# Value columns laid group last, four apart, in a windowed-attention and FFN kernel

## The chip, the cores and the metric

The kernel runs on one core of one Trainium2 chip. The metric is the device time of one launch in microseconds (us), the median of several executions. The engines of the core are TensorE (PE, with its weight loads shown apart as PEld), VectorE (DVE), ScalarE (ACT), GpSimd (POOL) and SyncE (SP), which here does nothing but issue DMAs; ACT issues some too. 16 DMA engines move the data of both queues.

## What is computed

`x` is (4, 2048, 256) in fp32, 8192 tokens in all. One transformer layer is applied:

```python
x = x + attn(layernorm(x), Wq, Wk, Wv, Wo)   # 16 heads of 16, token i sees tokens i-63 .. i
x = x + ffn(layernorm(x), W1, b1, W2, b2)    # ternary W1 (1024x256) and W2 (256x1024), relu
# attn: q, k, v = x @ W.T; softmax(q k / 4 + bias) v; then @ Wo.T
```

## The kernel before

Precision comes from splitting: a value is held as a high and a low f16 part, and products are summed over the parts. That holds for the projections, for the values (`vd[..., v, ...]`, v = 0 high, 1 low) and for the softmax weights (`th`, `tl`).

The tokens go in 16 chunks of 512. Each chunk takes 16 slots (`for n in SLOTS`), and every engine's program is written out slot by slot with the tables `A_T`, `A_Q`, `Q_DMA`, `V_DMA` and so on. Stage A (`a_t`, `a_qk`, `a_v`) of a chunk runs in the slots before its attention, attention takes one slot per unit of 4 query blocks of 4 heads (`scores(n)`, `exps`, `turn`, `low`), and stage C (`wo`, `c_t`, `c_f`, `c_y`: output projection and FFN) follows after it. PE thus mixes, in every slot, scores of this chunk with stage C of the last and stage A of the next.

The 16 heads are four groups g of four heads h, head 4g + h, each of 16 columns d. Attention of a group, `values(gg)`, multiplies with block-diagonal stationary operands: `vb[b]` has, on partitions 32h to 32h+31, the values of head h for 32 tokens in the columns of h, and zeros elsewhere, so that one 128x128 f16 load serves the four heads of group g with both parts. It is 36 matmuls (32 in a batch's first chunk), th and tl in turn, each of 96 columns save four of 64 and four of 32, and each with its own weight load.

The way of the values: PE writes a chunk's V in two banks (line 1042), ACT and DVE copy high and low parts to `vd` (lines 559 and 786; a row of `vd` is a token), and then SP spreads them to `vb` by `place_v` (line 304): 16 DMAs of 32 KB written per chunk, for m in 0..3 and h in 0..3. SP's queue is in order. Its DMAs per chunk in that order are

- 16 of `place_v` (V), from slot 17 counted from the chunk before; the first waits until DVE has written the low parts of V;
- 8 of `place_q` for t = 1 (line 284), slot 20, and 2 of `place_k` for t = 1 (line 263), slot 22, called k1 below: the keys of groups 2 and 3, which `scores` of group 2 need at slot 8 of the chunk. The matmul that waits there is the first of that slot, the mask of line 967 (line 963 in a batch's first chunk);
- 12 of `place_q` and 4 of `place_k` for t = 0, for the chunk that follows (lines 284, 266, 268).

ACT's queue issues meanwhile the spreading of the softmax denominators (`parked`, `rwide`, lines 464 and 470), the loads of `x` for the sixth chunk ahead (line 478, 512 KB, until x has been read) and the stores (line 475).

The rows of Wv are transposed on PE in the set-up, and `weights` on ACT and DVE copies them to `wT["v"]` (lines 495 and 679).

Of the kernel before, what the change touches and what calls it, by code (L numbers as in the profile page):

```python
# [14 lines left out]
WS = 256.0  # L15
# [107 lines left out]
def build(nc, x_d, wq_d, wk_d, wv_d, wo_d, w1_d, b1_d, w2_d, b2_d, identf_d, maskf_d, smask_d, kmask_d, out_d):  # L123
    f32, f16, b16 = mybir.dt.float32, mybir.dt.float16, mybir.dt.bfloat16
    ALU, ACT, AX = mybir.AluOpType, mybir.ActivationFunctionType, mybir.AxisListType
# [4 lines left out]
    with ExitStack() as ctx:  # L130
        def sb(name, shape, dt):
            return ctx.enter_context(nc.sbuf_tensor(name, shape, dt))
# [10 lines left out]
        wT = {n: [sb(f"w{n}{p}", [128, 2, 256], f16) for p in "hl"] for n in "qkvo"}  # L143
# [28 lines left out]
        qm = sb("qm", [128, 2, 16 * 128], f16)  # L172
        ks = [sb(f"k{g}", [128, 1 + g // 2, 64 + CH], f16) for g in range(4)]
        kw = [sb(f"kw{g}", [128, 16, 96], f16) for g in range(2)]
        vd = sb("vd", [128, 4, 4, 2, 4, 16], f16)
        vb = [sb(f"vb{i}", [128, 4, 4, 4, 2, 4, 16], f16) for i in range(3)]
        pr = [sb(f"p{i}", [128, 384], f32) for i in range(NP)]
        pt = [sb(f"pt{i}", [128, 384], f32) for i in range(3)]
        negm = [sb(f"negm{i}", [128, 4], f32) for i in range(4)]
# [17 lines left out]
        banks = [ctx.enter_context(nc.psum_tensor(f"ps{i}", [128, 512], f32)) for i in range(8)]  # L197
# [24 lines left out]
        s_ex, s_ahi, s_chi = sem("s_ex"), sem("s_ahi"), sem("s_chi")  # L222
# [17 lines left out]
        def a_bank(c, w):  # L240
            return banks[TURN["A", c, w - 8 * c][0]]
# [51 lines left out]
        @block.sync  # L293
        def _(e):
            def place_v(c, m):
                b = c % 3
                e.wait_ge(s_alo, 8 * c + 6)
                e.wait_ge(s_zv, min(c, 2) + 1)
                if c >= 3:
                    e.wait_ge(s_pv, 4 * (c - 1))  # L300
                for h in range(4):
                    src = vd[32 * m:32 * m + 32, :, :, :, h, :].rearrange("p t g v d -> p (t g v) d")
                    dst = vb[b][32 * h:32 * h + 32, m, :, :, :, h, :].rearrange("p t g v d -> p (t g v) d")
                    e.dma_start(dst, src).then_inc(d_v[b], 16)  # L304

            e.dma_start(xs[0][:, 0:2, :], x_t[0][:, 0:2, :]).then_inc(d_x[0], 16)
            e.dma_start(identf[:, :], identf_d).then_inc(d_id, 16)
            e.dma_start(kmask, kmask_d).then_inc(d_km, 16)
            e.dma_start(smask, smask_d).then_inc(d_s, 16)
            for t in range(2):  # L310
                e.dma_start(nat["q"][:, t, :], wq_d[128 * t:128 * t + 128].rearrange("(g r) d -> r g d", g=2)
                            ).then_inc(d_w["q"], 16)
            for n, d in (("k", wk_d), ("v", wv_d)):
                e.dma_start(nat[n], d.rearrange("(t p) d -> p t d", p=128)).then_inc(d_w[n], 16)
            e.dma_start(pr[1][:, :], maskf_d).then_inc(d_m, 16)
            e.wait_ge(s_bz, 1)
            for r in (0, 32):
                e.dma_start(bt[0][r:r + 1, :], b1_d.rearrange("(a n) -> a n", a=1)).then_inc(d_b, 16)
                e.dma_start(bt[1][r:r + 1, :], b2_d.rearrange("(a n) -> a n", a=1)).then_inc(d_b, 16)
            e.dma_start(n1, w1_d.rearrange("(t p) d -> p t d", p=128)).then_inc(d_w["1"], 16)  # L320
            e.dma_start(n2, w2_d.rearrange("(t p) f -> p t f", p=128)).then_inc(d_w["2"], 16)
            for n in SLOTS:
                for t in range(2):
                    c = spread(n, Q_DMA[t], A_Q[t] + 2)
                    if c is not None:
                        place_q(e, c, t, ((0, 1, 2, 3), (0, 1, 2, 3), (0, 1, 2, 3) if c or t else (2, 3)))
                    c = spread(n, K_DMA[t], A_K[t] + 2)
                    if c is not None:
                        place_k(e, c, t, (0, 1) if c or t else (1,))
                c = spread(n, V_DMA, 17)  # L330
                if c is not None:
                    for m in range(4):
                        place_v(c, m)
# [125 lines left out]
        def _(e):  # L459
# [31 lines left out]
            def weights(ws):  # L491
                for w in ws:
                    n, t = "qkvo"[w // 2], w % 2
                    e.wait_ge(s_wp, w + 1)
                    e.activation(wT[n][0][:, t, :], banks[4 + w % 4][:, 0:256], ACT.Copy,
                                 scale=WS * (0.25 if n == "q" else 1.0)).then_inc(s_whi, 1)

            def magnitudes(j):
# [55 lines left out]
            def a_v(c, u):  # L554
                w = 8 * c + 4 + u
                e.wait_ge(s_a, w + 1)
                if c >= 1:
                    e.wait_ge(d_v[(c - 1) % 3], 256 * ((c - 1) // 3 + 1))
                e.activation(vd[:, 2 * u:2 * u + 2, :, 0].rearrange("p t g h d -> p (t g) (h d)"),
                             a_bank(c, w)[:, :].rearrange("p (a b) -> p a b", b=64), ACT.Copy, scale=1 / WS).then_inc(s_ahi, 1)  # L560

            def o_copy(gg):
                e.wait_ge(s_pv, gg + 1)
# [12 lines left out]
            for n in SLOTS:  # L576
# [24 lines left out]
                c = stage_c(n, X_DMA)  # L601
# [3 lines left out]
                for u in range(2):  # L605
                    c = stage_c(n, OUT_DMA[u])
# [11 lines left out]
                for h in range(2):  # L618
                    c = stage_c(n, C_T[h] + 1)
                    if c is not None:  # L620
                        c_t(c, h)
                    for f in range(4):
                        c = stage_c(n, C_F[h] + f + 1)
                        if c is not None:
                            c_f(c, h, f)
                for t in range(2):
                    c = stage_a(n, A_T[t] + 1)
                    if c is not None:
                        a_t(c, t)
                    c = stage_a(n, A_Q[t] + 1)  # L630
                    if c is not None:
                        a_q(c, t)
                    c = stage_a(n, A_K[t] + 1)
                    if c is not None:
                        a_k(c, t)
                    c = v_at(n - 1, t)
# [4 lines left out]
                for u in range(2):  # L641
                    c = norm_at(n, A_NORM[u], N_NORM[u])
# [6 lines left out]
        def _(e):  # L649
# [24 lines left out]
            def weights(ws):  # L674
                for w in ws:
                    n, t, bank = "qkvo"[w // 2], w % 2, banks[4 + w % 4]
                    hi, lo, src = wT[n][0][:, t, :], wT[n][1][:, t, :], bank[:, 0:256]
                    e.wait_ge(s_whi, w + 1)
                    e.scalar_tensor_tensor(out=lo, in0=src, scalar=WS * (0.25 if n == "q" else 1.0), in1=hi,
                                           op0=ALU.mult, op1=ALU.subtract).then_inc(s_wlo, 1)  # L680
# [100 lines left out]

            def a_v(c, u):
                w = 8 * c + 4 + u
                hi, lo = (vd[:, 2 * u:2 * u + 2, :, v].rearrange("p t g h d -> p (t g) (h d)") for v in range(2))
                e.wait_ge(s_ahi, w + 1)
                e.scalar_tensor_tensor(out=lo, in0=a_bank(c, w)[:, :].rearrange("p (a b) -> p a b", b=64),
                                       scalar=1 / WS, in1=hi, op0=ALU.mult, op1=ALU.subtract).then_inc(s_alo, 1)

            def o_add(gg):
# [40 lines left out]
            for n in SLOTS:  # L830
# [27 lines left out]
                for u in range(2):  # L858
                    c = stage_c(n, C_WO[u] + 1)
                    if c is not None:  # L860
                        residual(c, u, f"wo{u}")
                    c = stage_c(n, C_T[u] + 1)
                    if c is not None:
                        c_t(c, u)
                    for f in range(4):
                        c = stage_c(n, C_F[u] + f + 1)
                        if c is not None:
                            c_f(c, u, f)
                    c = stage_c(n, C_Y[u] + 2)
                    if c is not None:  # L870
                        residual(c, u, f"y{u}")
                for t in range(2):
                    c = stage_a(n, A_T[t] + 1)
                    if c is not None:
                        a_t(c, t)
                    c = stage_a(n, A_Q[t] + 1)
                    if c is not None:
                        a_q(c, t)
                    c = stage_a(n, A_K[t] + 1)
                    if c is not None:  # L880
                        a_k(c, t)
                    c = v_at(n - 1, t)
# [4 lines left out]
                for u in range(2):  # L887
                    c = norm_at(n, A_STATS[u], N_STATS[u])
# [4 lines left out]
                    c = stage_c(n, C_STATS[u])  # L893
# [4 lines left out]
        def _(e):  # L898
# [80 lines left out]
            def values(gg):  # L979
                c, g = gg // 4, gg % 4  # L980
                e.wait_ge(s_lo, 4 * gg + 4)
                e.wait_ge(d_v[c % 3], 256 * (c // 3 + 1))
                if gg >= 1:
                    e.wait_ge(s_osum, gg)
                else:
                    e.wait_ge(s_alo, 6)
                k0 = 0 if c % PER_BATCH == 0 else -2
                for k in range(k0, 16):
                    i0, i1 = max(k, 0), min(k + 3, 16)
                    off, num = 64 * i0 + 32 * k + 64, i1 - i0  # L990
                    lhs = vb[(c if k >= 0 else c - 1) % 3][:, k % 4, k % 16 // 4, g].rearrange("p v h d -> p (v h d)")
                    for tt in (th, tl):
                        rhs = tt[gg % 2][:, off:off + 64 * num].rearrange("p (a b) -> p a b", b=64)[:, :, 0:32]
                        ins = e.matmul(pvbank[:, 32 * i0:32 * i1], lhs, rhs, start=(k == k0 and tt is th),  # L994
                                       stop=(k == 15), skip_group_check=True)
                ins.then_inc(s_pv, 1)
# [111 lines left out]
            for n in SLOTS:  # L1108
# [19 lines left out]
                for h in range(2):  # L1128
                    c = stage_c(n, C_WO[h])
                    if c is not None:  # L1130
                        wo(c, h)
                    c = stage_c(n, C_T[h])
                    if c is not None:
                        c_t(c, h)
                    for f in range(4):
                        c = stage_c(n, C_F[h] + f)
                        if c is not None:
                            c_f(c, h, f)
                    for t in range(2):
                        c = stage_c(n, C_Y[h] + t)  # L1140
                        if c is not None:
                            c_y(c, h, t)
                for t in range(2):
                    c = stage_a(n, A_T[t])
                    if c is not None:
                        a_t(c, t)
                    c = stage_a(n, A_Q[t])
# [49 lines left out]
```

## Time and profile before

| | |
|---|---|
| Median of 3 runs | 757.39 us (755.42 to 757.71) |
| The profiled execution | 753.48 us, its span 751.7 us |
| Mean granted TensorE clock | 0.955 of full speed |
| PE busy | 669.8 us (89%) |
| DVE, ACT, POOL busy | 609.6, 569.0, 556.7 us (81, 76, 74%) |
| DMA packets | 511041, of them 479684 under 512 bytes |

A busy share is a mean over stages. A matmul's own time in the trace is its way through the array (some 200 ns for 96 columns); what a matmul costs in a stream is the distance from one start to the next. A DMA-issuing instruction has a duration on its queue as well: the time until the queue takes up the next.

### The profile page before, as it was taken

To read this page: it belongs to the slowest core of one execution; us is meant where nothing else is said; L and a number is where in the kernel's file an instruction comes from. 1 tells how busy PE (TensorE), PEld (TensorE's weight loads), DVE (VectorE), ACT (ScalarE), POOL (GpSimd) and SP (SyncE) were. 2 spreads that over 40 slices of the span, in tenths; PEclk is the share of its full clock that TensorE was granted. 3 is DMA by queue.
4 is the path that set the end of the run, shared out by engine and by line. 5 is a ranking of instruction groups with operands and counts; after the bars stand their busy time and mean duration, and the time that the engine had idled before them with its cause. 6 is when DMAs were issued, how large, how long until landed. Compare 5 with 4: busy or idle time off the path is not lost.

```text
span 751.7 us, 23901 instructions
## 1 busy us (share of the span) xinstructions
PE 669.8 (89%) x8048; PEld 569.0 (76%) x8048; DVE 609.6 (81%) x1391; ACT 569.0 (76%) x2489; POOL 556.7 (74%) x823
## 2 busy tenths in 40 slices
PE   7588798998979899898989989898997999897888
PEld 5456687887868687786868878686886878786776
DVE  5679798896969889598978969798896989797844
ACT  5768797896878789597868959787785989877722
POOL 7367898795868779487877958687695888788741
PEclk9769899999999999899999999999999999999999
DMA  8766666576655757656575775557476465665110
GB/s 270 106 84 95 112 80 96 86 95 123 72 94 77 122 90 92 122 66 103 77 120 88 92 124 72 93 78 122 85 90 116 56 103 82 91 90 89 34 43 29
DMA packets 511041, 70.59 MB, mean 94 GB/s; under 512 B 479684, under 2 KB 502470, under 8 KB 510920
## 3 DMA queue, kind: packets, MB, share of 16 engines
q1 hardware_dynamic: 478456, 42.43, 45.2%
q10 hardware_dynamic: 32464, 26.63, 13.7%
q8 instruction: 65, 1.06, 0.6%
q14 instruction: 56, 0.46, 0.2%
HBM read 20.25 MB, written 9.44 MB: 39 GB/s over the span
## 4 chain that ended last, share of the span: by engine, by line
PE 53%; SPq 18%; DVE 9%; DMA 8%; POOL 5%; issue 5%; ACT 2%; ACTq 0%; POOLq 0%; DVEq 0%
PE ps L1095 12%; PE ps L994 9%; SPq L304 9%; SPq L284 9%; PE ps L974 7%; DMA k<-kst 7%; PE ps L1083 6%; PE ps L1056 5%; PE ps L1031 4%; PE ps L1042 4%; DVE negm L718 2%; POOL tl L419 2%; PE ps L967 2%; PE ps L1068 1%; POOL osum L391 1%
## 5 line engine op out<-in xcount | busy, mean ns | idle before, releaser
L520 ACT ACTIVATE p<-ps,negm 128x96 f32<-128x96 f32 x1024 | 335.6, 355 | 18.6 <-DVE negm L718 18.6
L419 POOL TENSOR_TENSOR tl<-pt,th 128x384 f16<-128x384 f32 x256 | 234.1, 914 | 20.7
L520 ACT ACTIVATION_READ_ACCUMULATOR p<-ps,negm 128x1 f32 x1024 | 227.1, 222 | 0.0
L718 DVE TENSOR_REDUCE negm<-ps 128x4 f32<-128x384 f32 x256 | 138.6, 542 | 95.4 <-PE ps L974 91.5
L417 POOL CAST th<-pt 128x384 f16<-128x384 f32 x256 | 129.1, 504 | 86.0 <-DVE pt L735 83.3
L735 DVE STREAM_TRANSPOSE pt<-p 128x384 f32<-128x384 f32 x256 | 143.3, 560 | 2.4 <-ACT p L520 2.2
L974 PE MATMUL ps<-k,qbd 128*128 128x96 f16 x1536 | 127.5, 210 | 0.0
L974 PEld LDWEIGHTS ps<-k,qbd 128*128 128x128 f16 x1536 | 107.7, 100 | 11.4 <-issue 0.4
L994 PE MATMUL ps<-th,vb 128*128 128x96 f16 (+1 forms) x1120 | 109.5, 213 | 1.9 <-issue 1.9
L994 PE MATMUL ps<-tl,vb 128*128 128x96 f16 (+1 forms) x1120 | 108.8, 213 | 0.0
L994 PEld LDWEIGHTS ps<-th,vb 128*128 128x128 f16 x1120 | 102.5, 105 | 2.2 <-issue 2.0
L994 PEld LDWEIGHTS ps<-tl,vb 128*128 128x128 f16 x1120 | 101.6, 105 | 0.0
L1083 PE MATMUL ps<-xTCh,w1T 128*128 128x256 f16 x512 | 97.6, 272 | 0.8 <-ACT xTCh L568 0.8
L564 ACT ACTIVATE ohalf<-ps 64x512 f32<-64x512 f32 x64 | 37.9, 592 | 72.1 <-PE ps L994 71.5
L573 ACT ACTIVATE hTh<-ps 128x512 f16<-128x512 f32 x128 | 78.7, 615 | 16.5 <-PE ps L1083 16.0
L827 DVE SCALAR_TENSOR_TENSOR hTl<-ps,hTh 128x512 f16<-128x512 f32 x128 | 86.8, 679 | 3.0 <-ACT hTh L573 3.0
L1083 PE MATMUL ps<-xTCl,w1T 128*128 128x256 f16 x256 | 69.8, 272 | 1.3 <-DVE xTCl L820 1.2
L967 PE MATMUL ps<-maskf,identb 128*128 128x256 bf16 x120 | 33.0, 275 | 42.0 <-DMA k<-kst 40.1
L1083 PE MATMUL ps<-xTCl,w1L 128*128 128x256 f16 x256 | 69.8, 273 | 0.0
L1095 PE MATMUL ps<-w2T,hTl 128*128 128x256 f16 x512 | 66.5, 273 | 0.2 <-DVE hTl L827 0.2
L1095 PE MATMUL ps<-w2T,hTh 128*128 128x256 f16 x512 | 66.5, 273 | 0.0
L974 PE MATMUL ps<-kw,qm 128*128 128x96 f16 x512 | 61.3, 211 | 0.0
(141 smaller groups left out, 1439.5 us busy)
## 6 DMA issues: line engine op xcount, KB each, us to landing
k<-kst SPq DMA_DIRECT2D x32, 288.0 KB, 3.7
vb<-vd SPq DMA_DIRECT2D x256, 32.0 KB, 2.9
rwide<-parked ACTq DMA_DIRECT2D x32, 256.0 KB
out<-x ACTq DMA_DIRECT2D x32, 256.0 KB, 2.9
qbd<-qs SPq DMA_DIRECT2D x254, 32.0 KB, 2.5
x<-in_L_attn_hidden ACTq DMA_DIRECT2D x15, 512.0 KB, 5.3
kw<-kst SPq DMA_DIRECT2D x31, 192.0 KB, 4.6
k<-kst SPq DMA_DIRECT2D x31, 144.0 KB, 4.2
```

The costliest lines, as they stand in the source:

```text
L284: e.dma_start(bass.AP(tensor=to[:, :, :].tensor, offset=(32 * h + v) * 4096 + 32 * h, ap=[[2 * 4096, 16], [128, 32], [1, 32]]), qst[t][32 ...
L417: e.tensor_copy(th[g % 2][:, o], pt[n % 3][:, :]).then_inc(s_hp, 1)
L419: e.tensor_tensor(tl[g % 2][:, o], pt[n % 3][:, :], th[g % 2][:, o], ALU.subtract).then_inc(s_lo, 1)
L520: ins = e.activation(p[:, 96 * u:96 * u + 96], bank[:, 96 * u:96 * u + 96], ACT.Exp, bias=m[:, u:u + 1], accum_out=r[:, u:u + 1])
L573: e.activation(hT[0][:, 2 * f:2 * f + 2, :].rearrange("p a b -> p (a b)"), c_bank(c, f"f{h}{f}")[:, :], ACT.Relu).then_inc(s_chi, 1)
L718: e.tensor_reduce(negm[n % 4][:, :], sbank[n % 3][:, 0:384].rearrange("p (a b) -> p a b", b=96), AX.X, ALU.max, negate=True).then_inc(s_mx, 1)
L735: e.transpose(pt[n % 3][:, :], pr[n % NP][:, :]).then_inc(s_tr, 1)
L827: e.scalar_tensor_tensor(out=lo, in0=c_bank(c, f"f{h}{f}")[:, :], scalar=0.0, in1=hi, op0=ALU.max, op1=ALU.subtract).then_inc(s_cdv, 1)
L974: ins = e.matmul(bank[:, 96 * u:96 * u + 96], to[:, g % 2, 128 * blk:128 * blk + 128], keys, start=(g < 2 and not first and m == 0 and u = ...
L994: ins = e.matmul(pvbank[:, 32 * i0:32 * i1], lhs, rhs, start=(k == k0 and tt is th), stop=(k == 15), skip_group_check=True)
L1083: ins = e.matmul(bank[:, o], w, xTC[xp][:, k, :], start=(xp + k == 0), stop=(xp + k == 2))
L1095: ins = e.matmul(bank[:, o], hT[hp][:, f, t * 128:(t + 1) * 128], w2T[:, f, :], start=False, stop=(f == 7 and hp == 1))
```

## The change

In `vd` and `vb` the group g becomes the last dimension, behind the head's columns d; high and low part, head and column stand ahead of it. A row of `vd` is then, for each token tile t and part v, 256 elements in the order (h, d, g), where it was (g, h, d) with the parts between. For a head h, all four groups and 16 columns of a part lie side by side: 64 elements, 128 bytes. Before they were runs of one group, 16 elements, 32 bytes. `place_v` names the same elements, in 8 runs of 128 bytes for each of 32 partitions instead of 32 runs of 32 bytes.

So that stage A writes V in that order at once, the columns of `wT["v"]` are put into the order (h, d, g) in the set-up, with writes four elements apart; the copies of V from PSUM to `vd` then have rows of 256 on both sides. The stationary operand of `values` is now read from `vb` with elements four apart (8 bytes) instead of side by side. The instructions of each engine, their order and their waits stay as they were.

```diff
-        vd = sb("vd", [128, 4, 4, 2, 4, 16], f16)
-        vb = [sb(f"vb{i}", [128, 4, 4, 4, 2, 4, 16], f16) for i in range(3)]
+        vd = sb("vd", [128, 4, 2, 4, 16, 4], f16)
+        vb = [sb(f"vb{i}", [128, 4, 4, 2, 4, 16, 4], f16) for i in range(3)]
...
-                    src = vd[32 * m:32 * m + 32, :, :, :, h, :].rearrange("p t g v d -> p (t g v) d")
-                    dst = vb[b][32 * h:32 * h + 32, m, :, :, :, h, :].rearrange("p t g v d -> p (t g v) d")
+                    src = vd[32 * m:32 * m + 32, :, :, h].rearrange("p t v d g -> p (t v) (d g)")
+                    dst = vb[b][32 * h:32 * h + 32, m, :, :, h].rearrange("p t v d g -> p (t v) (d g)")
...
-                    e.activation(wT[n][0][:, t, :], banks[4 + w % 4][:, 0:256], ACT.Copy,
+                    hi, src = wT[n][0][:, t, :], banks[4 + w % 4][:, 0:256]
+                    if n == "v":
+                        hi, src = hi.rearrange("p (a g) -> p g a", g=4), src.rearrange("p (g a) -> p g a", g=4)
+                    e.activation(hi, src, ACT.Copy,
...
-                e.activation(vd[:, 2 * u:2 * u + 2, :, 0].rearrange("p t g h d -> p (t g) (h d)"),
-                             a_bank(c, w)[:, :].rearrange("p (a b) -> p a b", b=64), ACT.Copy, scale=1 / WS).then_inc(s_ahi, 1)
+                e.activation(vd[:, 2 * u:2 * u + 2, 0].rearrange("p t h d g -> p t (h d g)"),
+                             a_bank(c, w)[:, :].rearrange("p (a b) -> p a b", b=256), ACT.Copy, scale=1 / WS).then_inc(s_ahi, 1)
...
-                hi, lo = (vd[:, 2 * u:2 * u + 2, :, v].rearrange("p t g h d -> p (t g) (h d)") for v in range(2))
+                hi, lo = (vd[:, 2 * u:2 * u + 2, v].rearrange("p t h d g -> p t (h d g)") for v in range(2))
...
-                    lhs = vb[(c if k >= 0 else c - 1) % 3][:, k % 4, k % 16 // 4, g].rearrange("p v h d -> p (v h d)")
+                    lhs = vb[(c if k >= 0 else c - 1) % 3][:, k % 4, k % 16 // 4, :, :, :, g].rearrange("p v h d -> p (v h d)")
```

DVE's part of the set-up and of `a_v` changes in the same way as ACT's.

## Rows read from the trace of the kernel before

**Rows 1.** The page: the span, and busy time, share and instructions of each engine

```profile
span 751.7 us, 23901 instructions
...
PE 669.8 (89%) x8048; PEld 569.0 (76%) x8048; DVE 609.6 (81%) x1391; ACT 569.0 (76%) x2489; POOL 556.7 (74%) x823
```

**Rows 2.** The waits of PE: us in total, times, the longest

```profile
PE ps L967 <- DMA k<-kst: 40.1, 12, 4.8
PE ps L963 <- DMA k<-kst: 12.2, 3, 4.6
```

**Rows 3.** Windows from one V burst to the next: length, busy by engine, clock, DMA share, GB/s

```profile
103.69:146.66 42.97, 40.27 (x501) 34.71 (x500) 36.62 (x85) 34.36 (x155) 34.27 (x51) 0.96 0.59 85
...
235.23:277.39 42.16, 38.59 (x494) 33.28 (x492) 36.65 (x85) 34.53 (x156) 33.61 (x51) 1.00 0.67 99
...
542.41:587.65 45.24, 40.61 (x496) 35.01 (x495) 36.79 (x85) 34.79 (x156) 33.63 (x51) 0.96 0.62 93
587.65:627.75 40.10, 38.60 (x494) 33.26 (x492) 36.00 (x83) 34.52 (x156) 33.64 (x51) 1.00 0.62 92
```

**Rows 4.** The timeline of SP's queue, chunks 8 and 13: start, us, DMAs issued

```profile
365.66 13.89 SPq L304 DMA_DIRECT2D vb<-vd  x16
379.65 8.06 SPq L284 DMA_DIRECT2D qbd<-qs  x8
387.83 1.47 SPq L263 DMA_DIRECT2D k<-kst  x2
...
587.65 14.00 SPq L304 DMA_DIRECT2D vb<-vd  x16
601.75 5.35 SPq L284 DMA_DIRECT2D qbd<-qs  x8
```

**Rows 5.** The chain that ended last, from 380 to 396 us: start, us, what

```profile
387.83 3.54 DMA k<-kst
...
391.50 0.32 PE ps L963
...
392.44 2.40 PE ps L994 x32
```

**Rows 6.** Lines 304, 284 and 263 by source line: ns of one issue, min/median/max

```profile
L304 SPq DMA_DIRECT2D vb<-vd x256: 585/668/3903, 34.3 to 679.6; - x128
...
L284 SPq DMA_DIRECT2D qbd<-qs x254: 585/630/3417, 17.4 to 687.0; - x127
...
L263 SPq DMA_DIRECT2D k<-kst x32: 567/584/611, 32.9 to 688.3; - x32
```

**Rows 7.** The page, DMA queues: packets, MB, share of 16 engines' span

```profile
q1 hardware_dynamic: 478456, 42.43, 45.2%
```

**Rows 8.** SP's queue (q1) in 370 to 374, 383.4 to 387.2 and 389.2 to 391.4 us

```profile
q1 hardware_dynamic: 4490, 0.14, 50.9%
...
q1 hardware_dynamic: 2838, 0.18, 47.3%
...
q1 hardware_dynamic: 261, 0.48, 94.0%
```

**Rows 9.** The timeline of ACT's queue in chunk 8

```profile
376.92 0.37 ACTq L478 DMA_DIRECT2D x<-in_L_attn_hidden  x1
```

**Rows 10.** The timeline of PE in one group of `values`: start, us, matmul

```profile
359.99 0.18 PE L994 MATMUL ps<-th,vb 128*128 128x32 f16 x1
360.02 0.18 PE L994 MATMUL ps<-tl,vb 128*128 128x32 f16 x1
...
360.27 0.21 PE L994 MATMUL ps<-th,vb 128*128 128x96 f16 x1
360.31 0.21 PE L994 MATMUL ps<-tl,vb 128*128 128x96 f16 x1
```

**Rows 11.** The chain from 330 to 400 us: a whole group of `values` at full clock

```profile
369.54 1.40 PE ps L994 x36
```

**Rows 12.** Groups of weight loads, shapes apart: busy us, mean ns of one, idle before

```profile
L994 PEld LDWEIGHTS ps<-th,vb 128*128 128x128 f16 x1120 | 102.5, 105 | 2.2 <-issue 2.0 <-POOL tl L419 0.2
...
L1020 PEld LDWEIGHTS ps<-identf,xnA 128*128 128x128 f32 x128 | 15.4, 147 | 0.7 <-DVE wvl L679 0.6
```

More of the change, by code:

```diff
@@ L677, in weights @@
                     hi, lo, src = wT[n][0][:, t, :], wT[n][1][:, t, :], bank[:, 0:256]
+                    if n == "v":
+                        hi, lo = (z.rearrange("p (a g) -> p g a", g=4) for z in (hi, lo))
+                        src = src.rearrange("p (g a) -> p g a", g=4)
                     e.wait_ge(s_whi, w + 1)
@@ L783, in a_v @@
                 w = 8 * c + 4 + u
-                hi, lo = (vd[:, 2 * u:2 * u + 2, :, v].rearrange("p t g h d -> p (t g) (h d)") for v in range(2))
+                hi, lo = (vd[:, 2 * u:2 * u + 2, v].rearrange("p t h d g -> p t (h d g)") for v in range(2))
                 e.wait_ge(s_ahi, w + 1)
-                e.scalar_tensor_tensor(out=lo, in0=a_bank(c, w)[:, :].rearrange("p (a b) -> p a b", b=64),
+                e.scalar_tensor_tensor(out=lo, in0=a_bank(c, w)[:, :].rearrange("p (a b) -> p a b", b=256),
                                        scalar=1 / WS, in1=hi, op0=ALU.mult, op1=ALU.subtract).then_inc(s_alo, 1)
```

## The prediction

> **What bounds the kernel now.** I read the page's first part, then PE's waits, then windows cut at the start of each V burst, then SP's queue, then the chain through one wait.
>
> PE is the busiest engine, 669.8 of 751.7 us, and DVE follows with 609.6 [rows 1]. Of the 82 us in which PE is idle, one cause holds 52.3: 40.1 us in 12 waits and 12.2 in 3 at the mask matmul of group 2, released by the DMA of k1 [rows 2]. That is one wait in nearly every chunk, 3.5 us on the mean, 4.8 at most. The windows show that PE loses nothing else of size. A full chunk costs PE 38.6 us of busy time where the granted clock was 1.00 [rows 3], and one whose clock fell costs about 40.5, since the clock drops to 0.5, the lower of its two levels, right behind a wait: the 32 matmuls of `values` after the one at 391.50 took 2.40 us [rows 5], where a whole group of 36 takes 1.40 [rows 11]. Over the 11 windows from 103.69 to 587.65 PE is busy for 442.2 us (40.2 each, first and last in [rows 3]), and 11 times 38.6 is 424.6: the low clock costs 17.6 us beside the waits.
>
> Why k1 is late shows in SP's queue. In chunk 8 the V burst starts at 365.66 (V's low parts have just been written), 16 V and 8 q issues take until 387.71, k1 is issued behind them at 387.83 [rows 4], lands 3.54 us later, and PE goes on at 391.50 [rows 5]. PE had been ready at 387.78, by its idle time of 3.72. So from the burst's start to k1 in place it is 25.7 us, and PE's own work fills 22.1. The wait is what the queue takes beyond that.
>
> **What the change does to SP's queue.** A V DMA had 32 partitions with 32 runs each, 1024 packets; now it has 256, and they hold four times the bytes. Over 256 DMAs 262144 of the queue's 478456 packets [rows 7] become 65536. Two things follow.
>
> *The issue itself.* Undisturbed issues take 668 ns for V (1024 runs), 630 for q (512 runs of 64 bytes) and 584 for k (128 long runs) [rows 6]. With 256 runs I put V at 600, by those three. Sixteen of them save 16 x 0.068 = 1.1 us a chunk.
>
> *The stalls.* Undisturbed, 16 V and 8 q issues with gaps of 40 ns would take 16 x 0.71 + 8 x 0.67 = 16.7 us. They take 22.0 in chunk 8, and 19.4 in chunk 13, behind which no x is loaded [rows 4]. So 2.7 to 5.3 us a chunk are single issues that stick, up to 3.9 us [rows 6]. In chunk 8 one falls together with the 512 KB of x issued at 376.92 on the other queue [rows 9]. How much of that lies on V's packets? From 370 to 374 us nearly all packets are V's: 4 us x 16 engines x 0.509 / 4490 = 7.3 ns for 32 bytes. In the q stretch it is 3.8 x 16 x 0.473 / 2838 = 10.1 ns, mostly for 64 bytes, and in the k1 stretch 2.2 x 16 x 0.94 / 261 = 127 ns for about 1800 bytes [rows 8]. The price is largely by the packet. 128 bytes should cost about 12 ns, an estimate between the second and third. One V DMA then holds each DMA engine for 16 x 12 = 0.2 us instead of 64 x 7.3 = 0.47, of 0.71 us from issue to issue. Behind a load of x the queue would be caught up sooner, but the load's own time stays. The bounds are no relief (0) and all of it (5.3). I take half, 2.6, since both V's backlog and x's transfer hold the queue and no row parts them.
>
> Together k1 lands 3.7 us earlier in a chunk (bounds 1.1 and 6.4). The waits of 52.3 us, each shortened by 3.7, leave about 4 us on the longest ones: a gain of 48. With no wait of size the clock has no reason to drop; of the 17.6 us I count 15. Before 103.69 and behind 587.65 I count no clock.
>
> *What is late next.* DVE is busy for 36.7 us of a chunk and PE will need 38.6 [rows 3]. That is little room, and DVE feeds the exponentials that free PE's score banks. That a chunk of 40.10 us ran with no other wait of size on PE [rows 3] shows that the others keep up to there; for the last 1.5 us no row does. I take off 0.4 us a chunk, 6 in all. Sum: 48 + 15 - 6 = 57.
>
> **What it does to the weight loads.** 2240 loads of `vb` now read elements 8 bytes apart. Today such a load costs nothing: in a group, 32-column matmuls start about 27 ns apart and 96-column ones 42 ns [rows 10], so a load takes at most some 27 ns and hides behind its neighbour. The 36 make 1.40 us [rows 11]. No row shows a strided load. A gain is excluded, since matmuls of 96 columns are already paced by their columns. If it takes up to 40 ns, only the eight narrow ones of a group grow, 8 x 13 ns x 64 groups = 7 us at most. The upper bounds: the only slower kind of load in the trace is that of f32, 147 ns in length against 105 [rows 12]. If a load's pace grew by those 42 ns, to 69, a group would take 36 x 0.069 = 2.5 us, or 70 us over 64 groups. If loads did not overlap at all, 36 x 0.105 = 3.8 us, it would be 153 us. I take zero: the room from 27 to 42 ns covers a read that is half again as slow, and the f32 load moves twice the bytes, which this does not.
>
> The trace is silent on strides, so the Trainium skill is weighed here. "SBUF — State Buffer" (Door 1, the note on cachelines) says that accesses within one 16-byte line run at full rate as long as two or more fall on a line; four f16 apart are exactly two. "TensorE: Matmul & The Clock Gate" (Weight-path perf modes) says that the fast load works packed or strided, but also that it reads 32 bits at a time instead of one element. If the second half of that ruled, a load would double to an estimated 54 ns, and a group would take 1.94 us: 35 us over all groups, and about 735 as the time. That stands as a rival below; no run here has shown it yet.
>
> **The rest.** The copies to `vd` have as many elements as before, with longer rows; the set-up's four strided copies happen once. The clearing of `vb` is the same size. I count nothing for them; the copies run under PE's work, and 0.1 us more in each would delay each V burst by as much.
>
> **The sum.** 753.5 (the profiled execution's own time) - 57 = 696.5. That execution was 3.9 us under the median of the runs, so the forecast is 757.4 - 57 = 700.
>
> **The rivals.**
> - *The stalls stay* (the queue sticks on the other queue's transfers alone). Then k1 gains 1.1 us a chunk: 16.5 us of waits and a few of clock, 738. For it: the longest issues coincide with x. Against: the price by the packet. "DMA: Bandwidth & Descriptors" (Why small descriptors are slow) of the Trainium skill speaks for it, and further: between SBUF and SBUF small descriptors cost nothing extra, so nothing but bytes would count, and the time would stay near 757. The rows disagree, with 4.4 bytes a ns at 32 bytes, 6.3 at 64 and 14 at 1800. Chance 0.12, with 0.03 of it for no change at all.
> - *Loads a little over the pace*, 45 to 60 ns a load. At 54 the group takes 1.94 us, plus 35 us against a gain of now 57 to 60: about 733. PE's own work between V burst and k1 grows too, so that waits vanish more surely. Chance 0.12.
> - *The weight loads become the bound*: over 62 ns a load (57 us over 64 groups are 0.89 us each, 2.29 / 36 = 64 ns) the kernel is slower than before. At 69 ns it is 757 + 70 - 63 = 764, at 105 ns 757 + 153 - 66 = 844. Middle 790. For it: the reads are no longer side by side, and every one of the 2240 is hit. Against: the room from 27 to 42 ns, and that bytes read are the same. Chance 0.14.
> - *DVE or ACT takes PE's place* at the higher rate: chunks stay at 40.1 as in window 587.65, instead of 38.6 plus 0.7. Then 13 chunks gain about 1 us less each: 713. It is in the likeliest case's range.
>
> **How the numbers follow.** Forecast case 0.62, its own range 686 to 718 (from all waits and 17.6 us of clock gone, 757 - 70 = 687, to chunks of 40.1 or a load at 40 ns). The range for 8 in 10 reaches to the stalls staying, 742, and takes in the loads a little over the pace; below it starts at 684. What is left out is the bound by weight loads and some of the edges. A difference of 0.3% (2.3 us) is about what a measurement of this kernel can tell from no change. Faster by more than that: 0.62 + 0.09 + 0.12 = 0.83. Within it: 0.03. Slower: 0.14.
>
> **What will show it.** SP's timeline: V issues with a median near 600 ns, and 16 V plus 8 q in 18 to 19 us. Packets of its queue near 282000. PE's waits for k1 under 10 us in total, the granted clock near 1.00 from 100 us on, chunk windows near 39.3 us. A group of `values` still at 1.40 us, with 27 ns between the narrow starts. The prediction falls if that group is over 1.5 us, or if the V and q issues still take 21 us.

## The result, and the profile after

The changed kernel takes 693.31 us (median of 4 runs, 691.04 to 696.39), the kernel before 756.4 us in the runs beside it. The ratio is 0.9175, with a 95% interval of 0.9127 to 0.9223. The forecast was 700. The profiled execution of the changed kernel took 696.39 us, with a span of 694.6. Some executions of the kernel before are slower than the rest; the ratios leave them out, so a ratio can say a little less than the medians beside it.

The page of the changed kernel, its span and busy times (against [rows 1]), and the packets of SP's queue (against [rows 7]):

```profile
span 694.6 us, 23901 instructions
...
PE 653.9 (94%) x8048; PEld 557.4 (80%) x8048; DVE 611.0 (88%) x1391; ACT 567.7 (82%) x2489; POOL 556.4 (80%) x823
...
q1 hardware_dynamic: 281848, 42.43, 38.7%
...
k<-kst SPq DMA_DIRECT2D x32, 288.0 KB, 4.0
```

The span fell by 57.1 us. PE's busy time fell by 15.9 of them and its idle time, span less busy, from 81.9 to 40.7. Packets fell by 196608, as counted. The last row is k1's time from issue to landing, 4.0 us where the page of before has 3.7: k1 did not land sooner after its issue, it was issued sooner.

PE's waits in the changed kernel (against [rows 2]):

```profile
PE ps L973 <- DMA k<-kst: 4.5, 5, 2.8
PE ps L969 <- DMA qbd<-qs: 4.3, 1, 4.3
PE ps L973 <- ACT p L523: 3.5, 4, 1.2
...
PE ps L1062 <- POOL oTl L399: 3.0, 2, 1.7
PE ps L1000 <- DVE osum L800: 1.6, 1, 1.6
...
PE ps L969 <- DMA k<-kst: 1.0, 1, 1.0
```

Of 52.3 us for k1, 5.5 are left. The other rows are small, 1 to 3.5 us each for ACT, POOL and DVE, and most of them stood in the kernel before at 1 to 3 us.

Windows from V burst to V burst (against [rows 3]; length, busy by engine, clock, DMA share, GB/s):

```profile
102.74:141.84 39.10, 38.90 (x502) 33.68 (x501) 36.66 (x85) 34.53 (x156) 34.54 (x52) 1.00 0.53 94
...
337.71:377.79 40.08, 39.12 (x496) 33.66 (x495) 36.83 (x85) 34.72 (x156) 33.61 (x51) 1.00 0.55 105
377.79:416.55 38.76, 38.70 (x494) 33.38 (x493) 36.47 (x85) 34.45 (x156) 33.65 (x51) 1.00 0.58 108
...
534.26:573.62 39.36, 38.70 (x494) 33.39 (x493) 36.02 (x83) 34.47 (x156) 33.55 (x51) 1.00 0.51 93
```

Full chunks take 38.8 to 40.1 us where all but one of [rows 3] took 42 to 46, at the full granted clock, and PE is busy for nearly all of it. PE is now the bound in the plain sense.

The timeline of SP's queue in chunks 8 and 13, counted from 0 as in [rows 4]:

```profile
337.71 11.66 SPq L304 DMA_DIRECT2D vb<-vd  x16
349.47 7.11 SPq L284 DMA_DIRECT2D qbd<-qs  x8
356.70 1.48 SPq L263 DMA_DIRECT2D k<-kst  x2
...
534.26 11.95 SPq L304 DMA_DIRECT2D vb<-vd  x16
546.30 6.22 SPq L284 DMA_DIRECT2D qbd<-qs  x8
```

The issue of V's DMAs by source line, ns min/median/max (against [rows 6]):

```profile
L304 SPq DMA_DIRECT2D vb<-vd x256: 585/611/1993, 35.7 to 623.4; - x128
```

From the burst's start to the end of q it is 18.9 us in chunk 8, where it was 22.0, and 18.3 in chunk 13, where it was 19.4. Chunk 8 is the slowest of the changed kernel. Over the ten chunks in which ACT's queue loads x during that stretch (3 to 12) the mean is 18.2 us where it was 22.1; over the full ones without such a load (2, 13, 14 and 15) it is 18.0 where it was 19.3. So the load of x hardly shows any more. The longest V issue is 1993 ns, where it was 3903.

The timeline of PE in one group of `values`, at its start and its end (against [rows 10]):

```profile
302.44 0.18 PE L1000 MATMUL ps<-th,vb 128*128 128x32 f16 x1
302.46 0.18 PE L1000 MATMUL ps<-tl,vb 128*128 128x32 f16 x1
...
303.82 0.19 PE L1000 MATMUL ps<-th,vb 128*128 128x32 f16 x1
303.86 0.18 PE L1000 MATMUL ps<-tl,vb 128*128 128x32 f16 x1
```

The chain that ended last, through a whole group of the changed kernel (against [rows 11]):

```profile
302.60 1.44 PE ps L1000 x36
```

The narrow matmuls (32 and 64 columns) start about 32 ns apart over the four pairs (27 before), the wide ones 42 as before, and the group takes 1.44 us instead of 1.40.

### The profile page after: what moved, and what is told of

Same layout as the page of the kernel before. It is cut to its first block, busy times and chain, and to the rows that moved or that the text cites. A ratio compares the mean times of both kernels' runs of the same rounds, so it can differ in the third digit from the quotient of the medians.

```text
span 694.6 us, 23901 instructions
## 1 busy us (share of the span) xinstructions
PE 653.9 (94%) x8048; PEld 557.4 (80%) x8048; DVE 611.0 (88%) x1391; ACT 567.7 (82%) x2489; POOL 556.4 (80%) x823
## 3 DMA queue, kind: packets, MB, share of 16 engines
q1 hardware_dynamic: 281848, 42.43, 38.7%
## 4 chain that ended last, share of the span: by engine, by line
PE 69%; SPq 7%; POOL 6%; DVE 6%; DMA 5%; ACT 4%; issue 3%; ACTq 0%; POOLq 0%; DVEq 0%
PE ps L1101 14%; PE ps L1089 11%; PE ps L1000 10%; PE ps L980 9%; PE ps L1037 8%; PE ps L1062 6%; PE ps L1048 4%; SPq L284 4%; DMA k<-kst 3%; SPq L304 3%; POOL tl L419 2%; PE ps L973 2%; PE ps L1074 2%; ACT p L523 2%; PE ps L1026 2%
## 5 line engine op out<-in xcount | busy, mean ns | idle before, releaser
L419 POOL TENSOR_TENSOR tl<-pt,th 128x384 f16<-128x384 f32 x256 | 234.4, 916 | 20.7
L980 PE MATMUL ps<-k,qbd 128*128 128x96 f16 x1536 | 125.6, 207 | 0.0
L980 PEld LDWEIGHTS ps<-k,qbd 128*128 128x128 f16 x1536 | 106.1, 99 | 11.1 <-issue 0.3
L1000 PE MATMUL ps<-th,vb 128*128 128x96 f16 (+1 forms) x1120 | 100.5, 205 | 2.2 <-DVE osum L800 1.6
L1000 PE MATMUL ps<-tl,vb 128*128 128x96 f16 (+1 forms) x1120 | 100.5, 205 | 0.0
L1000 PEld LDWEIGHTS ps<-th,vb 128*128 128x128 f16 x1120 | 96.4, 115 | 2.8 <-issue 1.7
L1000 PEld LDWEIGHTS ps<-tl,vb 128*128 128x128 f16 x1120 | 95.8, 115 | 0.0
L391 POOL TENSOR_TENSOR osum<-osum,rwide 128x512 f32<-128x512 f32 x32 | 40.6, 1268 | 22.1 <-DVE osum L800 21.4
```

Source lines behind the costliest of these rows:

```text
L419: e.tensor_tensor(tl[g % 2][:, o], pt[n % 3][:, :], th[g % 2][:, o], ALU.subtract).then_inc(s_lo, 1)
L980: ins = e.matmul(bank[:, 96 * u:96 * u + 96], to[:, g % 2, 128 * blk:128 * blk + 128], keys, start=(g < 2 and not first and m == 0 and u = ...
```

## The experiments

In four of them (quarter, half, step1 and step8) and in smallx part of the computation is left out or replaced, as their expectations say.

**quarter**: the packets of the changed kernel without its layout, and a quarter of its bytes.

```diff
 # the kernel before
-src = vd[32 * m:32 * m + 32, :, :, :, h, :]
-dst = vb[b][32 * h:32 * h + 32, m, :, :, :, h, :]
+src = vd[32 * m:32 * m + 32, 0:1, :, :, h, :]
+dst = vb[b][32 * h:32 * h + 32, m, 0:1, :, :, h, :]
```

> The kernel before with each V DMA cut to the first of four token tiles: 8 runs of 32 bytes per partition, 256 packets as in the changed kernel, but a quarter of its bytes, and the weights still read side by side. Three quarters of the values stay zero, so the output lacks them. If the packets of V set the queue's time: V issues near 611 ns, 16 V plus 8 q in about 17.5 us, and the time of the changed kernel less the cost of its strided loads, 688 to 694 us. If it was V's bytes, the time comes out clearly below the changed kernel's, since those bytes are a quarter. If the gain of the change came from anything but the V DMAs, this stays near 757.

688.9 us, ratio 0.9144 (0.9065 to 0.9224). The timeline of its SP queue, chunk 9:

```profile
371.53 11.49 SPq L304 DMA_DIRECT2D vb<-vd  x16
383.11 5.92 SPq L284 DMA_DIRECT2D qbd<-qs  x8
```

17.5 us, with V issues of 611 ns in the median; the changed kernel has 17.8 and 611. So the gain is that of V's DMAs and of their number of packets: with that number and a quarter of the bytes the time is that of the changed kernel within 4.4 us, of which the strided loads account for some 2.2 and the set-up for about one.

**half and pairs**: 512 packets for each V DMA, of 32 bytes in the one and 64 in the other. Half takes `0:2` where quarter takes `0:1`. Pairs is a layout between the two kernels, with all the work done; its weights lie two elements apart.

```diff
 # pairs, against the changed kernel
-vd = sb("vd", [128, 4, 2, 4, 16, 4], f16)
+vd = sb("vd", [128, 4, 2, 2, 4, 16, 2], f16)
...
-lhs = vb[...][:, k % 4, k % 16 // 4, :, :, :, g]
+lhs = vb[...][:, k % 4, k % 16 // 4, g // 2, :, :, :, g % 2]
```

> Half of the change: the groups go in pairs, so runs are 64 bytes (512 packets per V DMA) and the weights are read two apart. If engine time by the packet sets the stalls: 16 V plus 8 q in about 19 us, waits for k1 of 0 to 2 us per chunk, 697 to 712 us. If any run over 32 bytes is enough: as the changed kernel, 693. Load pace between 27 and 32 ns either way.

> The kernel before with each V DMA cut to two of four token tiles: 512 packets of 32 bytes, weights read side by side; half of the values stay zero and the output lacks them. The run with 64-byte runs had 512 packets of twice the bytes and took 698.3 us. If the packets decide: 693 to 698, V issues at 630 ns, 16 V plus 8 q in 18 to 18.3 us, and it lies above the quarter version (688.9) by its packets. If run length decides, since 32-byte packets are the costly kind: 715 or more.

Pairs took 698.3 us (ratio 0.9259, 0.9192 to 0.9326), half 693.3 (0.9256, 0.9184 to 0.9328). The timeline of SP's queue in pairs, chunk 9:

```profile
377.85 11.71 SPq L304 DMA_DIRECT2D vb<-vd  x16
389.66 6.65 SPq L284 DMA_DIRECT2D qbd<-qs  x8
```

PE's waits in half:

```profile
PE ps L967 <- DMA k<-kst: 12.6, 10, 3.5
```

In pairs it is 18.5 us from the burst's start to the end of q. In half the waits for k1 are 12.6 us, over twice the 5.5 of the changed kernel and a quarter of the 52.3 of before. Both times lie in the ranges expected if the packets decide. So 1024 packets a DMA give 753 to 757 us, 512 give 693 to 698, and 256 give 689 to 693. The effect is far from even: nearly all of the gain lies between 1024 and 512. The run of 32 bytes is not what is dear in itself, since half has it too.

**step1 and step8**: the changed kernel with other distances between the elements of the stationary operand, everything else the same.

```diff
-lhs = vb[...][:, k % 4, k % 16 // 4, :, :, :, g].rearrange("p v h d -> p (v h d)")
+lhs = vb[...][:, k % 4].rearrange("p t v h d g -> p (t v h d g)")[:, 0:1024].rearrange("p (a s) -> p a s", s=8)[:, :, 0]
 # step1: 0:128 and s=1
```

> The changed kernel with the stationary operand of values read from 128 elements side by side (the first of the tile, the wrong ones, so the attention output is wrong); DMAs as in the changed kernel. If the four-apart loads cost the 4 ns of pace seen on 32-column matmuls and no more: a group back at 1.40 us from 1.44, 64 x 0.04 = 2.6 us, so 690 to 692 us. Rival, strided loads cost nothing: 693.

> The changed kernel with the stationary operand read eight elements (16 bytes) apart, from the wrong elements. If a read of a 16-byte line that gives a single element is slower than one that gives two: load pace over 42 ns, up to 54 or 64, group of 36 at 1.9 to 2.3 us, time 715 to 745. Rival, the pace does not depend on the step: a group stays at 1.44 us and the time at 693.

Step1 took 692.2 us (0.9184, 0.9114 to 0.9255), which the total cannot tell from 693.3. Step8 took 723.7 us (0.9604, 0.9534 to 0.9673). The chain through one group in step1:

```profile
319.50 1.40 PE ps L1000 x36
```

The chain through one group in step8:

```profile
280.55 2.15 PE ps L1000 x36
```

The weight loads of step8 by source line, ns min/median/max:

```profile
L1000 PEld LDWEIGHTS ps<-th,vb x1120: 142/157/175, 50.1 to 690.5; 128*128 128x128 f16 x187
```

At eight apart the 36 matmuls start 60 ns apart on the mean (2.15 / 36): the load is then what sets the pace, for the wide ones too. So the pace of a load is at most 27 ns side by side, at most 27 at two apart (pairs), 32 at four and 60 at eight. With 42 ns for 96 columns, four apart was the last of these that hides. The 0.75 us more in each of four groups are 3.0 us a chunk; from one V burst to the next it is 41.6 us (349.69 to 391.27) where step1 has 38.9 (335.85 to 374.71), so 2.7 of them arrive in a full chunk. In the total it is 31.5 us. In the profiled executions it is 34.1, and 33.5 of these arise between the V bursts of chunks 2 and 15 (100.67 to 639.82 against 101.44 to 607.05); ahead of them and behind them the longer groups add next to nothing.

"SBUF — State Buffer" (Door 1, the note on cachelines) of the Trainium skill puts the edge between two accesses to a 16-byte line and one. The runs agree with that edge, 32 ns against 60, but not that four apart are quite free: they cost 5 ns more than side by side. Nor do they bear out what the same note draws from it, that a step of eight two-byte elements is still free. "TensorE: Matmul & The Clock Gate" (Weight-path perf modes) of the Trainium skill says that 32 bits are read at a time instead of one element, which by itself would have doubled the load as soon as elements lie apart; at two and at four apart it did not double.

**spare8 and spare4**: time of SP's queue alone.

```diff
 # the changed kernel, behind the 16 place_v DMAs of a chunk
+for i in range(8):        # spare4: 4
+    e.dma_start(spare[0:16, i, :], identf[0:16, 0:16]).then_inc(d_spare, 16)
```

> The changed kernel with 8 tiny DMAs (16 runs of 64 bytes from a constant to a spare tile that nothing reads) on SP's queue between each chunk's V and q DMAs, from the second chunk on. They take issue time, some 8 x 0.6 = 4.9 us a chunk, and next to no time of the DMA engines. If k1's lateness by SP's queue time is what cost the kernel before its 57 us: V burst to end of q in about 23 us, a wait for k1 of 3.5 to 5 us a chunk, the granted clock down behind it, 745 to 770 us. Rival, the gain came from freeing the DMA engines of packets: 693 to 705.

> As spare8 with 4 of them: 2.5 us later, so waits for k1 near 2 us a chunk. If the low clock comes only behind waits of about 2.7 us and more, as in the kernel before, the time rises by the waits alone, 693 + 15 x 2 = 715 to 725 us. Rival, every wait brings the low clock: 735 and more. Rival, no dependence on queue time: 693.

Spare8 took 786.9 us (1.0491, 1.0424 to 1.0557), spare4 727.3 (0.9685, 0.9616 to 0.9754). The timeline of SP's queue in spare8, chunk 7:

```profile
329.83 11.66 SPq L306 DMA_DIRECT2D vb<-vd  x16
341.53 6.10 SPq L340 DMA_DIRECT2D spare<-identf  x8
347.75 6.20 SPq L286 DMA_DIRECT2D qbd<-qs  x8
```

PE's waits in spare8:

```profile
PE ps L980 <- DMA k<-kst: 63.2, 12, 7.3
PE ps L976 <- DMA k<-kst: 12.5, 3, 4.7
```

DMAs that move next to nothing bring back all that the change had taken away and more: waits of 75.7 us for k1, and a mean granted clock of 0.939. The packets of SP's queue take 34.4% of the DMA engines' span there, less than the 38.7 of the changed kernel. So it is the queue's time ahead of k1 that PE pays for, not the load on the DMA engines. The size was missed: eight spare DMAs took 6.1 us, not 4.9, and the time came out 17 us over the range. In spare4 the waits are 35.6 us; 727.3 us is 2 over the range that rested on a clock that stays up, and the low clock did not need a wait of 2.7 us as I had expected. Two waits of spare4 in PE's timeline, the idle time in brackets:

```profile
419.07 0.34 PE L980 MATMUL ps<-maskf,identb 128*128 128x256 bf16 x1 [2.33 <-DMA k<-kst]
504.84 0.27 PE L980 MATMUL ps<-maskf,identb 128*128 128x256 bf16 x1 [2.23 <-DMA k<-kst]
```

The windows behind these two waits (length, busy by engine, clock, DMA share, GB/s):

```profile
419.10:422.10 3.00, 3.00 (x40) 2.96 (x41) 2.01 (x6) 0.14 (x2) 1.37 (x2) 0.51 0.58 75
504.90:507.90 3.00, 3.00 (x56) 2.87 (x57) 2.42 (x6) 1.18 (x6) 1.30 (x2) 1.00 0.55 70
```

Behind an idle time of 2.33 us the clock is at the lower level, 1.2 GHz, and 40 matmuls pass in 3 us; behind one of 2.23 us it is at 2.4 GHz and 56 pass. That is no edge, though. A longer wait in the kernel before, and the 3 us behind it:

```profile
260.43 0.27 PE L967 MATMUL ps<-maskf,identb 128*128 128x256 bf16 x1 [3.56 <-DMA k<-kst]
...
260.48:263.48 3.00, 3.00 (x56) 2.87 (x57) 2.40 (x6) 1.01 (x4) 0.18 (x1) 1.00 0.63 76
```

Behind 3.56 us of idle time the clock is at its full level there, and behind one of 3.60 us in spare8 (at 312.79) too, while in smallx one of 2.15 us (at 624.36) is followed by 0.51. The length of a wait alone does not say whether the clock falls.

**smallx and x_early_before**: whether V's packets make the long issues alone. In smallx the loads of x from the seventh chunk on are a quarter as large; in x_early_before they are whole and come five slots earlier.

```diff
 # smallx, in load_x, for c >= NX
-e.dma_start(xs[c % NX][:, :, :], x_t[c])
+e.dma_start(xs[c % NX][:, 0:1, :], x_t[c][:, 0:1, :])
 # x_early_before, and x_early on the changed kernel
-OUT_DMA, X_DMA = (23, 29), 36
+OUT_DMA, X_DMA = (23, 29), 31
```

> The kernel before with the loads of x from the seventh chunk on cut to the first of four token tiles (128 KB for 512), so the later chunks' input is partly stale and the output wrong. If the long issue behind each load of x is x's own transfer: that stall shrinks from 3 to about 1 us, 16 V plus 8 q in 19.5 instead of 21.3 us over ten chunks, 725 to 738 us. If V's packets alone make the stalls: 750 to 757.

> The kernel before with the load of x for the sixth chunk ahead issued 5 slots (some 12 us) earlier, just ahead of the V burst. If the long issue behind x's load is a fixed cost wherever it falls between V and k1, and x now lies ahead of it: 16 V plus 8 q in 19.5 to 20.5 us instead of 22 in the chunks with x, 728 to 742. Rival, it moves with x into the burst's first DMAs: 750 to 757.

Smallx took 729.1 us (0.9715, 0.9652 to 0.9778) and x_early_before 724.8 (0.9702, 0.9626 to 0.9778). The timeline of SP's queue in smallx, chunk 7:

```profile
310.96 15.02 SPq L304 DMA_DIRECT2D vb<-vd  x16
326.08 5.36 SPq L284 DMA_DIRECT2D qbd<-qs  x8
```

PE's waits in x_early_before:

```profile
PE ps L967 <- DMA k<-kst: 27.9, 12, 4.1
PE ps L963 <- DMA k<-kst: 6.4, 3, 2.4
```

Over chunks 3 to 12 V and q take 20.7 us in smallx and 20.3 in x_early_before, instead of 22.1, and the waits for k1 are 38.5 and 34.3 us instead of 52.3. The time of smallx lies in the range expected, that of x_early_before 3 us under its own. Moving one 512 KB load, with V's 1024 packets a DMA untouched, is worth 28 us by the medians and 22 by the ratio; making it a quarter as large, 25 and 21. So the long issues come from both: the other queue's transfers, and V's packets in their way. Neither rival as it stood (all on the packets, all on the other queue) was right.

The long issues of the kernel before, one by one, in chunk 8 and (last line) in chunk 13, where no x is loaded:

```profile
368.55 1.42 SPq L304 DMA_DIRECT2D vb<-vd  x1
...
376.46 2.37 SPq L304 DMA_DIRECT2D vb<-vd  x1
...
379.65 3.30 SPq L284 DMA_DIRECT2D qbd<-qs  x1
...
597.96 2.27 SPq L304 DMA_DIRECT2D vb<-vd  x1
```

The second, 2.0 to 2.5 us long, begins 10.2 to 10.9 us into each of the fourteen bursts from 103.69 on, with a load of x and without. It is not x's: smallx and x_early_before have it too (2.44 and 2.33 us in chunk 8), and in the changed kernel no issue that begins 9 to 11 us into a burst takes over 0.9 us. The third is what x adds: 2.5 to 3.9 us with x loaded meanwhile, and in chunk 8 1.37 in smallx and 1.53 in x_early_before. In the changed kernel's chunk 8 it is still 2.44 us, in its other full chunks 1.2 to 1.9.

**k_early and x_early**: whether something is left for the changed kernel. K_early issues the last four V DMAs of a chunk behind k1.

```diff
-                    for m in range(4):
+                    for m in range(3):
                         place_v(c, m)
+                c = spread(n, K_DMA[1], A_K[1] + 2)
+                if c is not None:
+                    place_v(c, 3)
```

> The changed kernel with the last 4 of a chunk's 16 V DMAs issued behind k1 instead of ahead of q. k1 lands 2.6 us earlier, and the last V lands (2.0 us from issue, against k1's 4.0) at about the time at which k1 landed before less 2 us. The waits for k1 that are left, 5.5 us in the profile, go: 686 to 690 us. Rival: they go, but PE waits for V in values instead, or the next engine's lag takes their place: 691 to 695.

> The changed kernel with the same earlier load of x. 1 to 2 us a chunk less from V burst to k1 (the q issue that sticks for 1.5 to 2.4 us), so the 5.5 us of waits for k1 go, 687 to 691 us. Rival, with waits already small nothing is left to gain: within 0.3% of 693.3.

K_early took 696.6 us (0.9283, 0.923 to 0.9336), x_early 691.8 (0.9247, 0.9201 to 0.9293). PE's largest row of waits in k_early:

```profile
PE ps L1003 <- issue: 6.3, 6, 2.8
```

PE's waits for k1 in x_early:

```profile
PE ps L973 <- DMA k<-kst: 3.4, 3, 2.8
```

In k_early no wait for k1 is left, but 6.3 us of waits stand at line 1003, the first matmul of `values`. The profile names no releaser for them. That it is the last V DMAs is read from the times, and not shown apart: at 279.12, behind 0.78 us of idle time, that matmul starts when the four DMAs whose issue ends at 277.11 should have landed, at 2.0 us from issue to landing. Its 696.6 us lie above both ranges expected. X_early leaves 3.4 us of waits for k1, and the 1.5 us by which its median lies lower are under what can be told from no change. Neither beats the changed kernel.

A note on medians: the kernel before had medians of 753.2 to 756.4 us beside the several groups of runs, so the ratios of different groups compare less well than the times of the variants do.

## Why the prediction was right

*What bounds the kernel.* Right: the wait for k1 was the loss, and the low clock behind it. Spare8 shows the cause from the other side, by queue time alone.

*The issue itself.* 600 ns was put, 611 was measured [rows 6 for before: 668], so 0.9 us a chunk instead of 1.1. The guess by the number of runs held: 611 at 256, 630 at 512 (pairs), 668 at 1024.

*The stalls.* Half of them was put as relief, 2.6 us, without a row that parted V's share from x's. V and q together gained 3.9 us in the chunks with x, 3.0 of it beyond the issues' own 0.9, and 1.3 in those without, 0.4 beyond; over chunks 2 to 15 it is 2.2. The middle came out nearly right for the mean, which is in part luck, and hid two cases. Where the prediction saw one issue fall together with the x issued at 376.92 there are two: that of 376.46, which sticks in every chunk, and that of 379.65, which is x's.

*A packet of 128 bytes* was put at 12 ns. The SP queue's packets in the changed kernel from 182 to 186 us, a stretch of V alone:

```profile
q1 hardware_dynamic: 1388, 0.17, 26.3%
```

4 x 16 x 0.263 us / 1388 = 12.1 ns.

*The waits left.* About 4 us were put, 5.5 are left: a gain of 46.8 against 48. 2.8 of them are the last wait for k1, in chunk 15, where no x is loaded and V and q gained only 1.2 us: it was 3.94 us.

*The clock.* 15 of 17.6 us were counted. All windows from 102.74 to 612.52 stand at 1.00, so the whole came back; some of it went to the loads again, and PE's busy time fell by 15.9 us on balance, 2 of them ahead of the first full chunk, where none was counted. "Right behind a wait" was said too broadly: two of the eleven windows, 235.23 and the one from 323.64, keep 1.00 behind waits of 3.56 and 3.26 us.

*What is late next.* 6 us were taken off. PE's idle time outside the waits for k1 went from 29.6 us (81.9 less 52.3) to 35.2 (40.7 less 5.5), so 5.6 us. The number is right by luck. It was put as 0.4 us in every chunk; in the windows from 102.74 to 612.52 PE is idle for 4.4 us, 2.6 of it for k1, so 1.8 in thirteen chunks, or 0.14 each. The other 3.8 us stand outside these windows, nearly all ahead of 102.74, in the set-up and the first chunks, where none was put. That DVE would be what is late was not right either: ACT, POOL and DVE share it.

*The weight loads.* Put at zero, with up to 7 us as the edge. The runs show 32 instead of 27 ns: 0.04 us in a group of 36, 0.02 at most in one of 32 (1.31 for 1.29), some 2.2 us in all. The forecast's room from 27 to 42 ns was the right measure, and the break-even that its sum gave, 64 ns (the 62 beside it does not follow from it), lies just above what eight apart cost: step8, at 60 ns, is still 4% faster than the kernel before.

*The rest* was put at nothing and costs a little. The copies of Wv in the set-up, by source line in the changed kernel, those of Wq for comparison:

```profile
L498 ACT ACTIVATE wqh<-ps x2: 362/364/367, 10.1 to 10.4; 128x256 f16<-128x256 f32 x2
...
L498 ACT ACTIVATE wvh<-ps x2: 752/794/837, 11.6 to 12.0; 128x256 f16<-128x256 f32 x2
...
L685 DVE SCALAR_TENSOR_TENSOR wql<-ps,wqh x2: 415/420/425, 10.5 to 10.9; 128x256 f16<-128x256 f32 x2
...
L685 DVE SCALAR_TENSOR_TENSOR wvl<-ps,wvh x2: 726/728/729, 12.3 to 12.9; 128x256 f16<-128x256 f32 x2
```

Written four apart, they take about twice as long, and the first V burst starts at 35.7 us where it started at 34.3 (line 304, first start, [rows 6] and above). That is 1.4 us, once. The start also moves between executions: it is at 34.2 to 35.1 us in the four other runs with the set-up as before and at 35.3 to 36.0 in the six others with the strided one. By the means of both kinds the copies cost 1.0 us.

*The sum.* 57 us were forecast between profiled executions, and 57.1 is the difference of the spans. The medians differ by 63: the profiled execution of the changed kernel was the slowest of its four, that of before lay under its median. The forecast of 700 is 7 us high by that.

*The rivals.* "The stalls stay" fell, but not because the other queue had no part: smallx and x_early_before give it 21 to 28 us. The rule that nothing but bytes counts between SBUF and SBUF, which the prediction took from "DMA: Bandwidth & Descriptors" (Why small descriptors are slow) of the Trainium skill, fell by quarter, which has a quarter of the bytes and no more than 4.4 us less time. The two rivals on the weight loads did not come, and step8 shows where the first of them begins.

*Left open.* Why the long V issues go away between 1024 and 512 packets, and not evenly. V's DMAs alone fill the DMA engines to 0.47 of 0.71 us at 1024 packets, which leaves little to catch up with behind a burst of the other queue; a limit on what may be outstanding would look the same. No run parts the two. That the second long issue stands at the same place in the burst with and without x speaks for such a limit; it is an argument and does not show it.

## What to carry to other kernels

Where a queue is in order, count what each DMA ahead of the awaited one costs the queue, issue and stalls, and not the bytes: here 16 DMAs of 32 KB delayed one that a whole engine waited for. Cutting the packets from 1024 to 512 a DMA did nearly all of it, and moving one large load of another queue out of that stretch did over a third as much without any change of layout; when the first is done, the second gives nothing that could be told from no change. A layout that makes the transfer cheap moves the stride to the reader: weight loads hid a step of four f16 behind 96 columns, and not one of eight.

## What had not been expected

- Copies on ACT and DVE that write f16 four elements apart take 794 and 728 ns for 256 columns, where side by side they take 364 to 382 and 415 to 420.
- A weight load paces at 60 ns when its f16 elements are 16 bytes apart, against 32 at 8 bytes, though the same 128 columns are loaded.
- A wait's length did not say whether the clock falls: it was at its lower level behind waits of 2.33 and 2.15 us, and at its full one behind 3.56 and 3.60 us.
- In every full chunk of the kernel before, one of V's last issues took 2.0 to 2.5 us, with or without a load of x on the other queue. In the changed kernel, and in chunk 8 of pairs and half, it is gone.
- One long issue some 3 us into a V burst stays whatever the packets: in chunk 8 1.42 us at 368.55 in the kernel before, and 1.57 us at 340.43 in the changed kernel.
